# Rotary embedding of the second layer's queries and keys in turned form, without TensorE transposes

## The reference, cut to what matters

```python
xn = _layernorm(x, axis=-1)                       # (4, 256, 256)
q = (xn @ Wq.T).reshape(B, S, 16, 16)             # 16 heads of 16
k = (xn @ Wk.T).reshape(B, S, 16, 16)
v = (xn @ Wv.T).reshape(B, S, 16, 16)
# _rope: x1, x2 are the first and last 8 values of a head
q, k = ([x1 * cos - x2 * sin, x2 * cos + x1 * sin] for both)
km = k.reshape(B, 8, 32, 16, 16).mean(axis=2)     # means of blocks of 32 keys
gate = einsum("bshd,bnhd->bhsn", q, km)           # picks 4 of 8 blocks
scores = einsum("bihd,bjhd->bhij", q, k) * 16 ** -0.5
```

## Time and profile before

| | us |
|---|---|
| runs | 677.92, 677.52, 677.00 (median 677.52) |
| span of the profiled execution | 675.4 (its own total is not given) |
| TensorE busy | 654.9 (97%) |
| VectorE busy | 500.7 (74%) |
| ScalarE busy | 417.7 (62%) |
| GpSimd busy | 298.5 (44%) |
| chain that ended last, TensorE's part | 78% |

### The profile page before, as it was taken

How to read it: one execution, slowest core, us unless ns; L and a number is a source line. 1 busy time by engine, 2 the same in 40 slices (tenths; PEclk the granted TensorE clock), 3 DMA queues, 4 the chain that set the end, 5 groups by cost and what they waited for, 6 DMA issues and landing times.

```text
span 675.4 us, 13827 instructions
## 1 busy us (share of the span) xinstructions
PE 654.9 (97%) x4756; PEld 573.9 (85%) x4756; DVE 500.7 (74%) x1425; ACT 417.7 (62%) x1084; POOL 298.5 (44%) x301
## 2 busy tenths in 40 slices
PE   5999999999999999999999998999999999999998
PEld 3777888898988899888888865556899999999997
DVE  6797877878778787887698788899577745645444
ACT  3766158888888888888865689998554222222221
POOL 1584146546464646452344418999532800400000
PEclk9999999999999999999999999999999999999999
DMA  8903034535535353444560000301100000000000
GB/s 316 378 5 102 1 112 128 167 116 165 165 112 191 100 180 115 123 129 125 210 257 1 1 1 1 112 1 53 75 1 1 2 17 1 1 16 1 2 16 16
DMA packets 26725, 59.43 MB, mean 88 GB/s; under 512 B 3146, under 2 KB 12748, under 8 KB 26272
## 3 DMA queue, kind: packets, MB, share of 16 engines
q1 hardware_dynamic: 23584, 50.35, 22.0%
q0 software_dynamic: 3072, 8.20, 3.7%
HBM read 48.24 MB, written 10.49 MB: 87 GB/s over the span
## 4 chain that ended last, share of the span: by engine, by line
PE 78%; DVE 10%; ACT 6%; issue 3%; POOL 2%; DMA 0%; ACTq 0%; POOLq 0%; DVEq 0%
PE bank L2292 10%; PE bank L2057 8%; PE bank L1991 7%; PE bank L2048 6%; PE bank L2343 5%; PE bank L2317 5%; PE bank L2077 4%; PE bank L2153 4%; PE bank L2068 4%; PE bank L1998 4%; ACT sb L1214 3%; PE bank L2119 3%; PE bank L2200 3%; PE bank L2359 3%; PE bank L1931 2%
## 5 line engine op out<-in xcount | busy, mean ns | idle before, releaser
L1073 ACT ACTIVATE sb<-bank,sb 128x256 f32<-128x256 f32 x128 | 59.6, 472 | 38.7 <-DVE sb L1578 33.5
L1281 ACT ACTIVATE h_parts<-sb 128x256 fp32r<-128x256 f32 x56 | 23.4, 418 | 76.5 <-DVE sb L1836 45.7
L2057 PE MATMUL bank<-sb 128*128 128x256 f32 x256 | 66.2, 381 | 0.0
L1578 DVE TENSOR_REDUCE sb<-bank 128x2 f32<-128x512 f32 x64 | 43.7, 683 | 27.1 <-PE bank L2057 26.6
L2292 PE MATMUL bank<-rounded,b_lo 128*128 128x256 f32 x224 | 63.0, 281 | 0.0
L2292 PE MATMUL bank<-rounded,b_hi 128*128 128x256 f32 x224 | 63.0, 281 | 0.0
L2292 PE MATMUL bank<-am_lo,b_hi 128*128 128x256 f32 x224 | 62.9, 281 | 0.0
L840 POOL DMA_INDIRECT expert_out<-sb x32 | 33.1, 1034 | 58.0 <-DVE sb L1520 44.2
L1080 ACT ACTIVATE sb<-sb 128x256 f32<-128x256 f32 x128 | 57.8, 505 | 0.1
L1827 DVE TENSOR_TENSOR sb<-sb,bank 128x256 f32<-128x256 f32 x56 | 23.4, 419 | 44.6 <-ACT sb L1238 44.5
L1238 ACT ACTIVATE sb<-bank 128x256 f32<-128x256 f32 x56 | 21.4, 382 | 53.3 <-PE bank L2292 53.3
(11 more groups left out here) (321 smaller groups left out, 1950.0 us busy)
## 6 DMA issues: line engine op xcount, KB each, us to landing
sb<-in_w_gate_up SPq DMA_DIRECT2D x32, 368.0 KB
sb<-in_w_down SPq DMA_DIRECT2D x32, 256.0 KB
sb<-in_w_pair SPq DMA_DIRECT2D x8, 704.0 KB
expert_out<-sb SPq DMA_DIRECT2D x1, 4096.0 KB, 23.5
sb<-expert_out SPq DMA_DIRECT2D x8, 512.0 KB, 6.8
sb<-in_w SPq DMA_DIRECT2D x1, 1792.0 KB, 12.9
sb<-in_b SPq DMA_DIRECT2D x1, 1792.0 KB, 7.4
sb<-in_sw_up SPq DMA_DIRECT2D x1, 1536.0 KB, 9.3
```

The costliest lines, as they stand in the source:

```text
L1073: act.activation(probs[:, u % 4, q, :], bank[3 + u % 2][:, q * S:(q + 1) * S], ACT.Exp, scale=-1.0, bias=row_min[:, u % 4, q:q + 1], accum ...
L1578: dve.tensor_reduce(row_min[:, u % 4, :], bank[3 + u % 2][:, :].rearrange("p (q n) -> p q n", q=QT), AX.X, ALU.min).then_inc(at_min, 1)
L2057: mm = pe.matmul(bank[3 + u % 2][:, q * S:(q + 1) * S], qb[i][:, h, b * S + q * P:b * S + (q + 1) * P], keys[:, h, b * S:(b + 1) * S], sta ...
```

## The change

Queries and keys are projected straight into the form with features on partitions: TensorE holds a 128 x 128 block of weights and streams 512 tokens (`project_heads`). There are eight such pieces, in the order of `PROJECTED`: block j (2 and 3 are keys, 0 and 1 queries), half c of the tokens. They use banks 4, 6 and 0 in turn. Values are projected as before (`project_values`), laid between. VectorE multiplies a piece by cosines and shuffles the two halves of each head within 32 partitions; GpSimd multiplies the shuffled copy by signed sines in place and adds both into `qkT`. The transposes, `qk_tok` and ScalarE's copies are gone. The tables now are 128 x 512 (`heads_rope`), loaded by a DMA of their own.

```diff
+HEAD_SWAP = [*range(8, 16), *range(8), *range(24, 32), *range(16, 24)]
+PROJECTED = ((2, 0), (3, 0), (2, 1), (3, 1), (0, 0), (1, 0), (0, 1), (1, 1))
+PROJECTED_BANK = (4, 6, 0)
...
             sp.wait_ge(at_pv, PAIRS * UNITS)
+            sp.dma_start(heads_rope.rearrange("p a b -> p (a b)"), t["heads_rope"]).then_inc(ab_in, 16)
             for i in range(LATE, NT):
                 results_in(i)
...
-            for i in range(NT):
-                pool.wait_ge(rope_mul, 3 * i + 3)
-                pool.tensor_tensor(qk_tok[:, i, :], rope_tmp[:, i % 2, 0, :], rope_tmp[:, i % 2, 1, :], ALU.add)\
-                    .then_inc(rope_add, 1)
-
+            pool.wait_ge(ab_in, 32)
+            for n, (j, c) in enumerate(PROJECTED):
+                plain, turned_ = (rope_tmp[:, n % 2, k, :] for k in range(2))
+                by_batch = turned_.rearrange("p (b s) -> p b s", s=S)
+                pool.wait_ge(rope_mul, 2 * n + 2)
+                pool.tensor_tensor(by_batch, by_batch, along(heads_rope[:, 1], (1, CH // S)), ALU.mult).then_inc(rope_add, 1)
+                pool.wait_ge(rope_add, n + 1)
+                pool.tensor_tensor(qkT[:, j, c * CH:(c + 1) * CH], plain, turned_, ALU.add).then_inc(qkT_out, 1)
+
+            pool.wait_ge(v_mm, NT)
...
                 if i == 2:
-                    act.wait_ge(ab_in, 16)
+                    act.wait_ge(ab_in, 32)
...
             for i in range(NT):
-                if i in (2, 4):
-                    x1_copies(9 + i // 2)
-                act.wait_ge(qkv_mm, i + 1)
+                if i in (2, 3):
+                    x1_copies(8 + i)
+                act.wait_ge(v_mm, i + 1)
...
-            for i in range(NT):
-                act.wait_ge(qkT_mm, i + 1)
-                act.activation(qkT[:, :, i * P:(i + 1) * P], bank[i % 4][:, :].rearrange("p (a n) -> p a n", a=4), ACT.Copy)\
-                    .then_inc(qkT_out, 1)
...
+            dve.wait_ge(ab_in, 32)
+            for n in range(len(PROJECTED)):
+                dve.wait_ge(qk_mm, n + 1)
+                at_least(dve, qkT_out, n - 1)
+                src = bank[PROJECTED_BANK[n % 3]]
+                dve.tensor_tensor(rope_tmp[:, n % 2, 0, :].rearrange("p (b s) -> p b s", s=S),
+                                  src[:, :].rearrange("p (b s) -> p b s", s=S), along(heads_rope[:, 0], (1, CH // S)), ALU.mult)\
                     .then_inc(rope_mul, 1)
...
+                dve.stream_shuffle(rope_tmp[:, n % 2, 1, :], src[:, :], HEAD_SWAP).then_inc(rope_mul, 1)
+                if n < 2:
+                    x1_low(10 + n)
...
-            dve.wait_ge(qkT_out, NT)
+            dve.wait_ge(qkT_out, 2 * KD)
...
+            def project_heads(n):
+                j, c = PROJECTED[n]
+                pe.wait_ge(turned_out, 10 + 2 * c)
+                at_least(pe, rope_mul, 2 * (n - 2))
+                if n == 2:
+                    pe.wait_ge(op_add, 7)
+                tile, cols = slice(j * P, (j + 1) * P), slice(c * CH, (c + 1) * CH)
+                terms = [(w, x, k) for w, x in ((w_qkvg_hi, x1T_hi), (w_qkvg_lo, x1T_hi), (w_qkvg_hi, x1T_lo)) for k in range(KD)]
+                for m, (w, x, k) in enumerate(terms):
+                    if m == 2 * KD:
+                        pe.wait_ge(xt_lo, 6 + 2 * c)
+                    mm = pe.matmul(bank[PROJECTED_BANK[n % 3]][:, :], r(w[:, k, tile]), r(x[:, k, cols]),
+                                   start=(m == 0), stop=(m == len(terms) - 1))
+                mm.then_inc(qk_mm, 1)
+
+            project_values(0)
+            project_values(1)
+            for n in range(len(PROJECTED)):
+                project_heads(n)
+                if n < 2:
+                    if n:
+                        project_values(2)
+                    turn1(10 + n, xn1, xn_done, NT + 2 * (2 + n) + 2)
+                    if n:
+                        project_values(3)
+                elif n > 3:
+                    project_values(n)
+
+            pe.wait_ge(rope_mul, 2 * len(PROJECTED))
             pe.wait_ge(v_out, NT)
...
                     pe.wait_ge(kmean_done, 1 + KD)
+                    pe.wait_ge(qkT_out, len(PROJECTED))
```

More of the change, by code:

```diff
@@ L177, in tables @@
     c1, s1 = np.cos(f1), np.sin(f1)
-    put("cos1", np.concatenate([c1, c1], -1).reshape(QT, P, D1).transpose(1, 0, 2))
-    put("sin1", np.concatenate([-s1, s1], -1).reshape(QT, P, D1).transpose(1, 0, 2))
+    heads_rope = np.concatenate([np.tile(np.concatenate(w, -1).T, (P // D1, 1)) for w in ((c1, c1), (-s1, s1))], 1)
     own = np.arange(S)[:, None] // CHUNK
@@ L218, in lay_out @@
     out = {"x": f["L0_attn_hidden_states"].reshape(TOK, D)}
-    out["consts"], out["consts_b"], out["slots"] = tables()
+    out["consts"], out["consts_b"], out["slots"], out["heads_rope"] = tables()
     out["consts"][:, CF["o_norm_col"][0]] = np.tile(f["L1_attn_o_norm_w"], P // D1)
@@ L466, in program @@
         w_hi, w_lo, w_rhi, w_rlo = ([rounded.take(4 * DR) for _ in range(2)] for _ in range(4))
+        heads_rope = Strip(region4, r4.at, 2 * S).take(2, S)
         keys = r4.take(2, TOK)
@@ L506, in program @@
         r2.take(NT * D)
-        qk_tok = r2.take(NT, 2 * D)
+        r2.take(NT * 2 * D)
         rope_tmp = r2.take(2, 2, 2 * D)
@@ L607, in program @@
         w3_in, ab_in, w2_in = sem("w3_in"), sem("ab_in"), sem("w2_in")
-        qkv_mm, rope_mul, rope_add, v_out, qkT_mm, qkT_out = (
-            sem(n) for n in ("qkv_mm", "rope_mul", "rope_add", "v_out", "qkT_mm", "qkT_out"))
+        qk_mm, v_mm, rope_mul, rope_add, v_out, qkT_out = (
+            sem(n) for n in ("qk_mm", "v_mm", "rope_mul", "rope_add", "v_out", "qkT_out"))
         kmean_set, kmean_done, blk_mm, blk_step = (sem(n) for n in ("kmean_set", "kmean_done", "blk_mm", "blk_step"))
@@ L1708, in _ @@
             scale_and_shift(NT - 1)
[L1711 to L1722, removed]
-                dve.tensor_tensor(by_sin[:, :, 0:half], src[:, :, half:D1], along(sin_t[:, 0:half], (1, 2 * H1)), ALU.mult)\
+            dve.wait_ge(ab_in, 32)
[5 more added lines that the diff above has]
+                                  src[:, :].rearrange("p (b s) -> p b s", s=S), along(heads_rope[:, 0], (1, CH // S)), ALU.mult)\
                     .then_inc(rope_mul, 1)
-                dve.tensor_tensor(by_sin[:, :, half:D1], src[:, :, 0:half], along(sin_t[:, half:D1], (1, 2 * H1)), ALU.mult)\
-                    .then_inc(rope_mul, 1)
+                dve.stream_shuffle(rope_tmp[:, n % 2, 1, :], src[:, :], HEAD_SWAP).then_inc(rope_mul, 1)
+                if n < 2:
+                    x1_low(10 + n)
             dve.wait_ge(v_out, NT)
@@ L2188, in _, with project_values @@
             pe.wait_ge(op_add, 6)
-            for i in range(NT):
-                if i in (2, 4):
-                    g = 9 + i // 2
-                    turn1(g, xn1, xn_done, NT + 2 * (g % 4) + 2)
+            def project_values(i):
                 pe.wait_ge(xt_lo, 5 + i // 2)
-                at_least(pe, rope_mul, 3 * (i - 1))
                 at_least(pe, v_out, i - 1)
@@ L2197, in _ @@
                 terms = [(x, w, k) for x, w in ((x1T_hi, w_qkvg_hi), (x1T_lo, w_qkvg_hi), (x1T_hi, w_qkvg_lo)) for k in range(KD)]
-                for part, (a, b) in enumerate(((0, 2 * D), (2 * D, 3 * D + E1))):
-                    for n, (x, w, k) in enumerate(terms):
-                        mm = pe.matmul(bank[4 + 2 * (i % 2) + part][:, 0:b - a], r(x[:, k, tile]), r(w[:, k, a:b]),
-                                       start=(n == 0), stop=(n == len(terms) - 1))
-                mm.then_inc(qkv_mm, 1)
@@ L2203, in _ @@
-            for i in range(NT):
-                pe.wait_ge(rope_add, i + 1)
-                at_least(pe, qkT_out, i - 3)
-                for j in range(4):
-                    mm = pe.transpose(bank[i % 4][:, j * P:(j + 1) * P], qk_tok[:, i, j * P:(j + 1) * P], ident)
-                mm.then_inc(qkT_mm, 1)
-            pe.wait_ge(rope_mul, 3 * NT)
+                for n, (x, w, k) in enumerate(terms):
+                    mm = pe.matmul(bank[5 + 2 * (i % 2)][:, 0:D + E1], r(x[:, k, tile]), r(w[:, k, 2 * D:3 * D + E1]),
+                                   start=(n == 0), stop=(n == len(terms) - 1))
```

8 lines of the change are left out of this document (5 added, 3 removed).

## The result

| kernel | median us | lowest to highest | runs |
|---|---|---|---|
| before | 677.52 | 676.78 to 677.92 | 5 |
| changed | 680.32 | 678.77 to 681.25 | 5 |

The ratio is 1.0042, 95% interval 1.0030 to 1.0054: slower by 2.8 us. The changed kernel's profiled execution is the one of 680.32, with a span of 678.5 (before 675.4): 3.1 us to account for.

A forecast was written before the change was run, and what follows sets the result against it. TensorE, busy 97% of the span, was taken as the bound. Transposes -3.41, stalls +1.05, old waiting -0.25 and waiting for GpSimd's chain +3.4 summed to +0.8 us: 678.3 us, range 676.4 to 680.9.

The forecast's parts named there:

- Removed and kept work: TensorE before the fills: 32 transposes (3.41 us) go, products stay as many; TensorE free at 379.0.
- The two stalls: TensorE's projections: 0.45 us waiting for VectorE's low part, 0.6 us before the third product; 1.05 us together.
- GpSimd's piece: GpSimd's sine multiply and add per projected piece: 2.59 us, bounds 2.37 and 2.79, eight pieces 20.7 us.
- The fills' start: First low-rank fill waits for VectorE's last shuffle, starting at 382.4, 0.8 us later than before; TensorE idle from 379.0.
- The block means: VectorE's subtract, reduction and two products before the block scores: done at 386.9, 1.2 us before needed, no stall.
- Tables and DMA: One more 256 KB DMA on SP's queue: costs nothing, hidden in 12 us; below 2 us if that cover were gone.
- The sum: All terms over the whole kernel: +0.8 us, giving 678.3 us.
- The likeliest case: GpSimd's chain delays the fills, as in the sum: 678.3 us, own range 677.3 to 679.3, chance 0.64.
- Rival B: The pause before the fills slows TensorE afterwards: 2.4 us more, at most 2.5, giving 680.7 us; chance 0.20.
- My own sign for it: Sign of a slowed TensorE: the fills' 512-column matmuls stand 0.46 us apart at first instead of 0.23.
- Rival A: GpSimd's chain does not bind; fills start at 379.0, 2.6 us sooner, giving 674.9 us; chance 0.13.
- Rival C: GpSimd's two passes cost their upper bound without slowed TensorE: +1.6, 679.1 us; inside the first case's range, no own chance.

The follow-up runs named there:

- the moved table: Changed kernel with both rotary tables five elements (20 bytes) further on in SBUF: 678.51 us, ratio 1.0014 to the kernel before.
- The early fills: Changed kernel whose first fills use other banks and no longer wait for VectorE's last shuffle: 678.18 us, ratio 1.0020 to the kernel before.
- the plain product moved: Changed kernel with tables moved 20 bytes and the add's cosine-product input also placed five elements off: 678.02 us, ratio 1.0007 to the kernel before.

## Why the prediction's sum was right and its number low

*Removed and kept work: right.* Products and values took what the sum gave them: TensorE is free at 379.11 + 0.25 = 379.36, a distance of 19.09, forecast 379.0, 19.1. A pair of 512 columns with held weights takes 0.46 us, six 1.4 as before.

*The two stalls: right together, the first half as long.* The low part came late (the pair of 362.39 is followed at 363.09, 0.24 more than its 0.46; 0.45 forecast) and the third product waited 0.44 on its own beside a late start (0.6 forecast). That product is done at 369.5, a distance of 9.2 (forecast 9.1).

*GpSimd's piece: right in the sum, wrong in its parts.* 2.63 measured, 2.59 forecast. The multiply was mis-sized, 1.30 and not 1.09, and so was the hand-over: I took it from the first layer, 1.23 + 1.36 us, while in the pair itself it is nearly hidden. With the multiply that I assumed a piece is 2.42, as the moved table shows; my lower bound (2.37) was nearer to that than my value. Two errors of about 0.2 us cancelled. The estimate by the Trainium skill's GPSIMD Engine Reference (Elementwise, side-by-side cycle accounting), 1.12 us an instruction, fits the 1.09 with the moved table but neither the 1.30 nor the add's 1.28. The Trainium skill's advice (GPSIMD Engine Reference, Engine selection), two inputs on VectorE, was the right one here: 676.11 against 680.19.

*The fills' start: right.* Distance 22.85, forecast 22.5; pause 3.61, forecast 3.4; the release is VectorE's shuffle, and GpSimd has no idle time from piece 2 to 7.

*The block means: right in place, not in size.* Without the slow clock the block scores start at 28.53, and VectorE's two products of the means, 1.34 us from 385.32 in that trace (0.76 in the earlier trace rows), end about 1.0 before it (forecast 1.2). They were drawn out beside GpSimd's last add, as I said, and also beside the copy behind it, which I had not counted. The early fills showed that this chain is the next wait.

*Tables and DMA: nothing seen*, as forecast: the distances are explained without them.

*The sum.* In the executions in which the clock holds the changed kernel takes 677.65 us (median of four, before 676.97): +0.7, where the sum says **+0.8**. The likeliest case's mechanism was right. That its size fits to 0.1 is in part luck: the fills start 1.17 us later than before and not 0.8, and the spans of these four are 1.0 us longer (medians 675.7 and 674.7). What an execution takes outside its span is 1.8 us here and 2.2 before, by the medians; I had carried 2.1 unchanged. Nothing here shows why it shrank. In the first measurement the one execution at 1.00 took 678.77, 1.25 above before.

*Rival B: weight and price too low.* I had it at 0.20, since "the rows show only that 6.9 is [enough] and that pauses under 1 us are not", and took it as a thing that happens or does not. It happened in 12 of 17 executions, so the median carries it. As an on-top cost I took 2.4 us; it was 1.57 in the first profile, of an execution at 0.997, and 3.1 for those at 0.994 or 0.995, above the bound of 2.5 that I had from the pace at the start. The forecast of 678.3 is therefore 2.0 us low, and the range (to 680.9) held the result only through B, a case that I had at 0.20: that the result lies in the range is luck as much as insight. My own sign for it was right: I said 0.46 apart instead of 0.23 for a matmul, and pairs of them are 0.86 apart instead of 0.46. The granted-clock column did show it here, 0.77, though at the start it read 1.00 at half the pace; so my doubt whether it would be seen was empty.
The Trainium skill (TensorE: Matmul & The Clock Gate, Why this matters for your kernels) warned of idle gaps between bursts, and its section What's actually happening says that at a kernel's start the place of the transition differs from run to run of one kernel. The executions agree with the first, slowed in 12 of 17, and show the same kind of difference in the middle of a kernel, with pauses of 3.60 and 3.61 us in either kind.

*Rival A* fell: GpSimd's chain binds, and leaving its multiply out gives 675.60 (674.9 forecast for A, which assumed no pause at all; 0.71 us stay). *Rival C* did not come, since the longer multiply was paid back by the hand-over.

## What to carry to other kernels

An operation that is moved off the busy engine is free only while the chain that takes it makes its pieces as fast as the busy engine does; here 2.63 us a piece against 2.14 (a product and a value tile, 1.41 + 0.73) made all 3.41 us of removed transposes into waiting, and one pass put on the other engine, with the wait moved to where the data are wanted, turned a loss of 0.4% into a gain of 0.2%. Before a pause of TensorE is taken for what it lasts, add what the clock may take afterwards: in these kernels pauses of 2.05 us and more cost another 0.6 to 3 us in many executions, and pauses of 1.29 us and less none. When a wait is moved, follow every consumer to the next one, or the pause only moves. And compare executions at the same clock, over several of them: the changed kernel's four at 1.00 are 0.7 us above the kernel before, its median 3.2.

## What the runs showed of the hardware that I had not expected

- One kernel, one pause of 3.60 us, two outcomes: granted clock 0.77 and 0.80 and fills of 7.24 us in one profile, 1.00 and 5.69 us in the other. With pauses of 2.8 us the same (1.00 with the table moved, slowed with the plain product moved too). A single profile cannot tell what such a pause costs.
- In the slowed profile the first three pairs after the pause start 0.57 and 0.46 apart at first (383.12, 383.69, 384.15) and only then 0.80 to 0.86: the slow stretch begins about 1 us after TensorE is back at work, and it is over by 388.
- A sine table 20 bytes further on in SBUF makes GpSimd's multiply of 128x512 take 1.093 instead of 1.29 us, each of the eight. Moving the add's plain input likewise changes nothing (1.280 and 1.285).
